# Token stage of a vision tower: three pixel buffers instead of two, and its eight groups written out instead of looped

## The reference

```python
x = img.reshape(B, C, h, P, w, P)                       # 64 images, 14 x 14 patches of 16 x 16 x 3
x = jnp.transpose(x, (0, 2, 4, 3, 5, 1)).reshape(B, h * w, P * P * C)
x = _layernorm(x, ln1_g, ln1_b)                         # over the 768 values of a patch
x = jnp.einsum('bnp,pd->bnd', x, W_proj) + b_proj       # 768 -> 192
x = _layernorm(x, ln2_g, ln2_b)                         # over 192
x = jnp.concatenate([cls, x], axis=1) + pos_embedding
...
h = h + attention(layernorm(h))    # 12 heads, relative positions, 198 tokens an image
h = h + ffn(layernorm(h))          # shared MLP and two of eight experts
```

## Time and profile before

| | |
|---|---|
| median of 3 runs | 5148.42 us (5146.3 to 5152.68) |
| the profiled execution: its time, its span | 5149.14 us, 5147.4 us |
| busy over the span | PE 4691.5 us (91%), DVE 3364.0 (65%), ACT 2283.2 (44%), POOL 562.3 (11%) |
| mean granted clock of TensorE | 0.954 of full speed |
| token stage | from the start to 496 us, where the first instructions of the attention stage stand |
| pixels read | 24 transfers of 1568 KB |

### The profile page before, as it was taken

The page is one execution under the profiler, slowest core; times in us unless marked ns, Lnnn a source line. Parts: engine busy times, 40 slices in busy tenths (PEclk is TensorE's granted clock), DMA queues, the critical chain, the costliest instruction groups (busy, mean ns, idle before and its releaser), DMA issues. The chain is left out here.

```text
span 5147.4 us, 91556 instructions
## 1 busy us (share of the span) xinstructions
PE 4691.5 (91%) x30810; PEld 4419.7 (86%) x30810; DVE 3364.0 (65%) x9549; ACT 2283.2 (44%) x6372; POOL 562.3 (11%) x530
## 2 busy tenths in 40 slices
PE   4775799899899989989989998998999699999999
PEld 4775599899889889989988998998999599999999
DVE  4555566666666766666666666676667477777776
ACT  2443555455555545545555555554554122222222
POOL 1122100000000000000000000000000133333333
PEclk8887799999999999999999999999999799999999
DMA  6452000000000000000000000000000100000000
GB/s 140 97 124 61 13 1 1 1 20 1 1 20 1 1 2 20 1 1 20 1 1 16 6 1 1 20 1 1 11 1 1 38 19 18 18 18 18 18 18 18
DMA packets 65157, 99.50 MB, mean 19 GB/s; under 512 B 3763, under 2 KB 60674, under 8 KB 61120
## 3 DMA queue, kind: packets, MB, share of 16 engines
q1 hardware_dynamic: 61312, 90.31, 7.0%
q0 software_dynamic: 944, 2.42, 0.3%
q10 hardware_dynamic: 2560, 2.36, 0.2%
HBM read 65.88 MB, written 29.20 MB: 18 GB/s over the span
## 5 line engine op out<-in xcount | busy, mean ns | idle before, releaser
L643 ACT ACTIVATE att_prob<-att_s,att_npeak 99x198 f32<-99x198 f32 x1536 | 640.1, 422 | 1221.4 <-DVE att_npeak L816 1175.5
L816 DVE TENSOR_REDUCE att_npeak<-att_s 99x2 f32<-99x396 f32 x768 | 436.0, 568 | 892.3 <-PE att_s L988 890.2
L971 PE MATMUL att_o<-att_probT,att_vx 99*96 99x198 f32 (+1 forms) x3072 | 683.2, 345 | 1.3 <-ACT att_probT L633 1.3
L988 PE MATMUL att_s<-att_kx,att_qx 96*99 96x198 f32 (+1 forms) x3072 | 657.4, 336 | 3.3 <-DVE att_xres L782 2.5
L1356 PE MATMUL ffn_y<-ffn_down,ffn_hidden 128*128 128x192 f32 x3564 | 634.8, 328 | 6.7 <-DVE ffn_acc L1268 4.8
L1356 PEld LDWEIGHTS ffn_y<-ffn_down,ffn_hidden 128*128 128x128 f32 x3564 | 585.6, 190 | 28.4 <-DVE ffn_acc L1268 27.4
L971 PEld LDWEIGHTS att_o<-att_probT,att_vx 99*96 99x96 f32 (+1 forms) x3072 | 509.5, 182 | 42.4 <-issue 32.7
L988 PEld LDWEIGHTS att_s<-att_kx,att_qx 96*99 96x99 f32 (+1 forms) x3072 | 517.1, 168 | 18.4 <-issue 4.4
L806 DVE TENSOR_SCALAR att_prob<-att_prob,att_total 99x198 f32<-99x198 f32 x1536 | 458.9, 342 | 26.9
L1134 POOL TENSOR_TENSOR ffn_hidden<-ffn_relu 128x384 f32<-128x384 f32 x462 | 379.4, 827 | 708.6 <-ACT ffn_relu L1163 400.2
L1163 ACT ACTIVATE ffn_relu<-ffn_h 128x384 f32<-128x384 f32 x231 | 113.3, 490 | 706.2 <-PE ffn_h L1345 705.9
(11 more groups left out here) (201 smaller groups left out, 9368.6 us busy)
## 6 DMA issues: line engine op xcount, KB each, us to landing
tok_pixels<-in_x SPq DMA_DIRECT2D x24, 1568.0 KB
ffn_hid<-hidden SPq DMA_DIRECT2D x34, 288.0 KB, 2.9
att_xres<-hidden SPq DMA_DIRECT2D x8, 1188.0 KB
hidden<-att_xres SPq DMA_DIRECT2D x8, 1188.0 KB
out_hidden<-ffn_acc SPq DMA_DIRECT2D x33, 288.0 KB, 2.3
hidden<-tok_rows SPq DMA_DIRECT2D x8, 1176.0 KB
att_oT<-in_L_attn_qkv_w ACTq DMA_DIRECT2D x1, 1536.0 KB, 11.4
tok_posb<-in_L_tok_pos_embedding POOLq DMA_DIRECT2D x1, 1176.0 KB, 42.6
```

The source lines that it names most:

```text
L643: ins = nc.scalar.activation(prob[:, i % 2, h, :], s_bank[i % 2][0:HALF, h * NTOK:(h + 1) * NTOK], ACT.Exp, bias=npeak[:, i % 2, h:h + 1], ...
L816: nc.vector.tensor_reduce(npeak[:, i % 2, :], s_bank[i % 2][0:HALF, 0:2 * NTOK].rearrange("p (h k) -> p h k", h=2), AX.X, ALU.max, negate= ...
L971: ins = nc.tensor.matmul(o_bank[j % 2][0:M, 0:NTOK], vx[:, p % 2, 2 * b + k, v0:v0 + M], probT[:, j % 2, k * NTOK:(k + 1) * NTOK], start=( ...
L988: ins = nc.tensor.matmul(s_bank[i % 2][0:HALF, h * NTOK:(h + 1) * NTOK], qx[0:K, p % 2, head, q0:q0 + HALF], kx[0:K, p % 2, head, b * NTOK ...
```

## The change

`pixels` gets three buffers and as many semaphores; group g uses buffer g % 3. SP issues three loads at the start and then, after the pixels of group g have been read, the load of g+3. The programs of SP, ACT and DVE in this stage are written out for eight groups instead of looped over pairs. In the last group DVE leaves out the statistics of pixels, their aggregation, scale and shift, and ACT the square root that belongs to them; the pretended arrival goes. PE and POOL keep their loops, and the other stages are as they were.

```diff
+    SLOTS = 3
-        pixels = m.sb("pixels", [P, 2, CH, XROW])
+        pixels = m.sb("pixels", [P, SLOTS, CH, XROW])
...
-                load(0, 0)
-                load(1, 1)
-                with sp.Fori(0, (GROUPS - 2) // 2) as pair:
-                    gg = pair * 2
-                    for s in range(2):
-                        sp.wait_ge(normed_made, (gg + s + 1) * SIDE)
-                        load(gg + s + 2, s)
-                        store(gg + s, s)
-                sp.sem_inc(pixels_in[0], 16 * CH)
-                for s in range(2):
-                    store(GROUPS - 2 + s, s)
+                for g in range(SLOTS):
+                    load(g)
+                for g in range(GROUPS):
+                    if g + SLOTS < GROUPS:
+                        sp.wait_ge(normed_made, (g + 1) * SIDE)
+                        load(g + SLOTS)
+                    store(g, g % 2)
...
-                with act.Fori(0, GROUPS // 2) as pair:
+                for g in range(GROUPS):
+                    s = g % SLOTS
...
+                    if g + 1 < GROUPS:
                         deviation1(g + 2)
-                        act.wait_ge(mv2_made, g + 1)
+                    act.wait_ge(mv2_made, g + 1)
...
-                with dve.Fori(0, GROUPS // 2) as pair:
-                        dve.wait_ge(pixels_in[1 - s], gg * (8 * CH) + 16 * CH * (s + 1))
-                            if wv < SIDE:
-                                ins = statistics1(1 - s, wv)
+                for g in range(GROUPS):
+                    s, more = g % 2, g + 1 < GROUPS
+                    if more:
+                        dve.wait_ge(pixels_in[(g + 1) % SLOTS], 16 * CH * ((g + 1) // SLOTS + 1))
+                        if wv < SIDE and more:
+                            ins = statistics1((g + 1) % SLOTS, wv)
...
+                    if more:
                         dve.wait_ge(normed_made, (g + 1) * SIDE)
                         aggregate(st, mv1, stat1, mv1_made)
-                        aggregate(st, mv2, stat2, mv2_made)
+                    aggregate(st, mv2, stat2, mv2_made)
+                    if more:
                         scale_shift1(st, g + 2)
...
-                        dve.wait_ge(rows_out[s], gg * 8 + PRIMED)
+                    if g >= 2:
+                        dve.wait_ge(rows_out[s], 16 * (g // 2) + PRIMED)
```

More of the change, by code:

```diff
@@ L110, in tokens_stage @@
         y_bank = [m.bank(f"y{v}") for v in range(2)]
-        pixels_in = [m.sem(f"pixels_in{s}") for s in range(2)]
+        pixels_in = [m.sem(f"pixels_in{s}") for s in range(SLOTS)]
         consts_in, weights_in, ident_made = m.sem("consts_in"), m.sem("weights_in"), m.sem("ident_made")
@@ L132, in _, with load @@
                     sp.sem_inc(s, PRIMED)
-                def load(g, s):
+                def load(g):
                     for c in range(CH):
-                        sp.dma_start(pixels[:, s, c, :], x_rows[c, :, bass.ds(g * GB, GB), :]).then_inc(pixels_in[s], 16)
+                        sp.dma_start(pixels[:, g % SLOTS, c, :], x_rows[c, :, g * GB:(g + 1) * GB, :]
+                                     ).then_inc(pixels_in[g % SLOTS], 16)
                 def store(g, s):
                     sp.wait_ge(rows_made, g + 1)
-                    sp.dma_start(hid_rows[:, bass.ds(g * GB, GB), :], rows[:, s, :, :]).then_inc(rows_out[s], 16)
-                load(0, 0)
-                load(1, 1)
-                with sp.Fori(0, (GROUPS - 2) // 2) as pair:
-                    gg = pair * 2
-                    for s in range(2):
-                        sp.wait_ge(normed_made, (gg + s + 1) * SIDE)
-                        load(gg + s + 2, s)
-                        store(gg + s, s)
-                sp.sem_inc(pixels_in[0], 16 * CH)
-                for s in range(2):
-                    store(GROUPS - 2 + s, s)
+                    sp.dma_start(hid_rows[:, g * GB:(g + 1) * GB, :], rows[:, s, :, :]).then_inc(rows_out[s], 16)
+                for g in range(SLOTS):
[5 more added lines that the diff above has]
+                    store(g, g % 2)
                 for s in range(2):
@@ L172, in _ @@
                 deviation1(1)
-                with act.Fori(0, GROUPS // 2) as pair:
[L174 to L188, removed]
+                for g in range(GROUPS):
+                    s = g % SLOTS
+                    act.wait_ge(shift1_made, g + 1)
+                    normalise(s, 0, g * SIDE)
+                    for wv in range(SIDE):
+                        v, t = wv % 2, g * SIDE + wv
+                        if wv + 1 < SIDE:
+                            normalise(s, wv + 1, t + 1)
+                        act.wait_ge(turned, t + 1 + PRIMED)
+                        for i in range(2):
+                            ins = nc.scalar.activation(patchT[:, v, 3 * i:3 * i + 3, :],
+                                                       t_bank[v][i][:, 0:3 * P].rearrange("p (k n) -> p k n", k=3),
+                                                       ACT.Copy)
+                        ins.then_inc(patchT_made, 1)
+                    if g + 1 < GROUPS:
                         deviation1(g + 2)
-                        act.wait_ge(mv2_made, g + 1)
-                        nc.scalar.activation(rstd2[:, :, :], mv2[:, :, 1:2], ACT.Sqrt, bias=eps[0:P, :]).then_inc(sd2_made, 1)
+                    act.wait_ge(mv2_made, g + 1)
+                    nc.scalar.activation(rstd2[:, :, :], mv2[:, :, 1:2], ACT.Sqrt, bias=eps[0:P, :]).then_inc(sd2_made, 1)
             @block.gpsimd
@@ new lines, in _ @@
+                for g in range(GROUPS):
+                    s, more = g % 2, g + 1 < GROUPS
+                    st = Steps(dve, dve_step, 2 + g * PER_GROUP)
+                    if more:
+                        dve.wait_ge(pixels_in[(g + 1) % SLOTS], 16 * CH * ((g + 1) // SLOTS + 1))
+                    dve.wait_ge(rows_normed, g + PRIMED)
+                    for wv in range(SIDE + 1):
+                        t = g * SIDE + wv - 1
+                        if wv:
+                            dve.wait_ge(projected, t + 1)
+                            nc.vector.tensor_tensor(y[:, wv - 1, :], y_bank[(wv - 1) % 2][0:P, 0:DIM], bias[:, :], ALU.add
+                                                    ).then_inc(y_made, 1)
+                        if wv < SIDE and more:
+                            ins = statistics1((g + 1) % SLOTS, wv)
+                            if wv == SIDE - 1:
+                                st.did(ins)
+                        if wv:
+                            dve.wait_ge(y_made, t + 1 + PRIMED)
+                            st.did(nc.vector.bn_stats(stat2[:, wv - 1, :], y[:, wv - 1, :]))
+                    if more:
@@ L288, in _ @@
                         dve.wait_ge(normed_made, (g + 1) * SIDE)
                         aggregate(st, mv1, stat1, mv1_made)
-                        aggregate(st, mv2, stat2, mv2_made)
+                    aggregate(st, mv2, stat2, mv2_made)
+                    if more:
                         scale_shift1(st, g + 2)
-                        dve.wait_ge(sd2_made, g + 1)
-                        st.did(nc.vector.reciprocal(rstd2[:, :, :], rstd2[:, :, :]))
-                        st.settle()
@@ L295, in _ @@
-                        dve.wait_ge(rows_out[s], gg * 8 + PRIMED)
[L296 to L301, removed]
+                    dve.wait_ge(sd2_made, g + 1)
@@ new lines, in _ @@
+                    st.did(nc.vector.reciprocal(rstd2[:, :, :], rstd2[:, :, :]))
+                    st.settle()
+                    if g >= 2:
+                        dve.wait_ge(rows_out[s], 16 * (g // 2) + PRIMED)
+                    for wv in range(SIDE):
+                        ins = nc.vector.tensor_scalar(rows[:, s, wv, :], y[:, wv, :], mv2[:, wv, 0:1], rstd2[:, wv, :],
+                                                      ALU.subtract, ALU.mult)
+                        if wv == SIDE - 1:
+                            ins.then_inc(rows_normed, 1)
@@ L303, in _ @@
+                    assert st.n == (PER_GROUP if more else PER_GROUP - 2), st.n
             @block.tensor
```

## The result

The changed kernel took 5157.42 us (median of 20 runs, 5153.79 to 5161.05), the kernel before 5146.55; the ratio is 1.002, with a 95% interval of 1.0014 to 1.0027. The profiled execution has a span of 5159.1 us. One of the 20 runs of the kernel before took 10713 us, which a median hardly feels. Forecast were 5075 us and a gain of 74. The measurement shows a loss of 11.

What follows compares the result with a forecast made beforehand. PE was taken as the bound, plus 9.10 us a group waiting on late pixels. Savings of 65.5 + 1.5 + 7 = 74.0 us from 5149.14 gave 5075.1, stated as 5075 us, range 5064 to 5092.

Steps and rivals of the forecast that it cites:

- Third buffer: Token stage: loads issued a group earlier remove six of DVE's pixel waits, 77.1 us together; 65.5 us saved.
- the first rival: Start of token stage: three loads share instead of queue, load 1 comes 28.5 us later, total 5103.6 us; 7%.
- Last group: End of token stage: 14 aggregations of unneeded pixel statistics leave the path to the row instructions; 1.5 us saved.
- the template: Old token stage's seventh group window, whose pixel wait was already satisfied: 43.45 us, taken as the model for groups after.
- The granted clock: Group boundaries of the token stage: PE's fall to half clock may cost less; 0 to 14 us gained, 7 taken.
- POOL beside DVE, and both beside the loads: Token stage: POOL's row instructions, DVE's statistics and pixel traffic now coincide without stretching; cost 0.
- The contention rival: Token stage: pixel traffic, POOL and DVE together stretch DVE or transfers, part of the wait returns; 5092 to 5138 us; 8%.
- the lock of the Trainium skill: Port pair shared by DVE and GpSimd, held exclusively: POOL's 11.8 us a group would fall on DVE, 5153 us; 1%.
- Code fetch within the token stage: Written-out DVE and ACT programs need 14 or 15 instruction packets; 0 to 10 us lost, 0 taken.
- The rival of fetches behind pixel packets: Token stage: DVE's and ACT's straight-line code packets queue behind loads, 108 us on the path, 5183 us; 3%.
- Attention and experts must not change by more than some us: Sign to look for in the later stages: their times stay as before within some us.

Runs made afterwards that it cites:

- 8: Changed kernel with 8 small memsets added at the head of DVE's program: 5075.1 us, ratio 0.9868 to the kernel before.
- 64: Changed kernel with 64 small memsets added at the head of DVE's program: 5073.99 us, ratio 0.9858 to the kernel before.
- 100: Changed kernel with 100 small memsets added at the head of DVE's program: 5075.24 us, ratio 0.9868 to the kernel before.
- 112: Changed kernel with 112 small memsets added at the head of DVE's program: 5123.43 us, ratio 0.9961 to the kernel before.
- 128: Changed kernel with 128 small memsets added at the head of DVE's program: 5161.05 us, ratio 1.0032 to the kernel before.
- the loop of 268: Changed kernel with 116 memsets, DVE's experts loop cut from 284 to 268 instructions by leaving out the gates' norming: 5062.91 us, ratio 0.9833.

## Why the prediction was wrong, point by point

- **Third buffer, 65.5 us**: right. All six waits went and the first stayed, at 15.09 us. Load 1 was no later (DVE went on at 65.96 instead of 65.91), so the loads do not share; the first rival falls.
- **Last group, 1.5 us**: right. The last window is 1.51 us shorter than the template (41.94 against 43.45). From the end of the last column's statistics to the group's first row instruction it is 1.85 us, where the kernel before has 3.16. The 14 aggregations left take 1.03 us, and DVE then waits 0.37 for ACT's square root.
- **The granted clock, 7 us**: right in kind, too large. Seven windows take 297.8 us; the template's 43.45 seven times is 304.2. The 6.3 us between them hold the last group's saving too, as the last window ends at its first L295. The six windows before it take 255.9 us against 260.7: the clock gave 4.8, within the bounds of 0 to 14; that it would be half of them was a guess. The windows are not alike, as forecast, but alternate: 43.2 at a mean clock of 0.92, 42.1 at 0.96, as the fall lasts 6.8 us at one boundary and 3.4 at the next. At no boundary did it fail to come, as I had thought possible for some. Windows at the first boundary, at the second, and behind it:

```profile
102.80:109.40 6.60, 5.57 (x22) 5.34 (x23) 5.42 (x18) 5.19 (x8) 2.14 (x1) 0.50 0.88 190
...
147.20:150.40 3.20, 3.20 (x16) 3.06 (x16) 3.16 (x11) 2.68 (x6) 0.00 (x0) 0.50 0.92 202
150.60:155.00 4.40, 4.40 (x34) 4.36 (x34) 2.94 (x10) 2.81 (x5) 4.40 (x1) 1.00 0.86 186
```

  The prediction misread one row. It has the fall at the last boundary of before 0.2 us after PE started again. But a grant of 0.91 over the 3.5 us up to 429.40 means 0.6 us of half clock in them, so the fall came at 428.8, 0.4 us before PE started at 429.18. A fall behind PE's start is seen only after the change, at the second boundary, where it was the short one. There PE started at 147.02, the fall came at 147.1, and the first project took 2.77 us where the template has 4.14:

```profile
147.02 2.47 PE L318 MATMUL tok_t<-tok_ident,tok_normed 112*128 112x112 f32 x12 [4.73 <-ACT tok_normed L166]
149.28 2.77 PE L330 MATMUL tok_y<-tok_w,tok_patchT 128*112 128x192 f32 x12
```

- **The three together**: 65.5, 4.8 and 1.5 us, less 0.7 by which the first window begins later (103.03 instead of 102.33), are the 71.1 us by which the token stage is shorter. 74 were forecast.
- **POOL beside DVE, and both beside the loads, 0**: right. In the group from 231 to 273 us, which has all three at once, L232 takes 412 ns and L215 5906, against 412 and 5897. The contention rival falls, and the lock of the Trainium skill (SBUF — State Buffer, section "SBUF: two separate sides") is again not seen for these instructions. The prediction says that the trace does not agree with the page; that is too strong, as L232 reads one tile and so need not meet the page's condition.
- **Code fetch within the token stage, 0 of 0 to 10 us**: right. 14 or 15 packets were forecast, 11 came up to 425 us (13 by 490), and neither DVE nor ACT has an issue wait there. The forecast divided by 88 working instructions a packet. In this stage the two programs have 965 and 355 instructions of all kinds, and 1320 over 128 is 10.3. The rival of fetches behind pixel packets falls too: the kernel did become slower and by fetches of code, but in the experts stage, which moves no pixels.
- **"Attention and experts must not change by more than some us"**: the step that failed. It stood among the signs to look for, and the sum has it as a zero for which no row is given. I priced the fetching of the code that is written out and not what its length does to the code behind it. In its place the runs show 82 to 85 us: 5.65 us in 15 turns of a loop whose 284 instructions had moved by 95 places of 128. With that undone, the forecast of 5075 stands against 5073.99, 5075.1 and 5075.24. That it is met to 1 us is in part luck: the gain against the kernel before of the same round is 73.1, 70.4 and 70.3 us, where 74 were forecast.

The rule that I cited bears on just this. The Trainium skill, Runtime: NRT & Kernel Launch, section "Instruction fetch mechanics", says that a taken branch whose target is not among the pages held forces a fetch before execution goes on. By that rule every loop that the change does not touch had to be asked whether it still is held; I used it only for the loops that the change removes. The trace agrees with the rule in kind: stalls at the branch's target, 3.0 and 1.7 us. It differs in the unit, which the section gives as 16 KiB blocks for each engine: the packets of q14 are 8192 bytes, and 128 instructions are one turn of the pattern.

What stays open: that three packets are kept and four are not is read from the packet counts and from the places tried (8, 64, 100, 112, 128 and the loop of 268); how the buffer replaces its contents was not tried. In a bad place five packets come per turn, one more than the loop covers; I take the fifth for the one behind the loop, which is argued only. It fits their times: three come at the head, one 30 us later, and one 7 us before the next head. And 3.4 us that the changed kernel lost late in the attention stage are not explained; 2.5 of them had come back at the start of the experts stage, so the loss of 84 us is not touched.

## What to carry to other kernels

A change that alters the number of instructions in one stage moves every later loop of that engine against the ends of the fetched packets; where a loop is about as long as what the engine keeps (here 284 instructions of DVE, by the count kept from 101 places of 128), it can lose a few us in every turn far from the diff. When a gain vanishes in code that was not touched, compare the instruction packets of the two profiles and the "issue" waits at loop heads, and move the code by a few instructions in a stretch where the engine waits anyway: 8 were enough here, 82 us for nothing. And take a verdict on a change only after that, since the same edit is 73 us faster or 11 us slower by its place alone.

## What was not expected of the hardware

A loop of 284 DVE instructions is fetched once, or with five packets of 8192 bytes in every turn, by its place alone: 152 packets in the whole kernel or 226. In the changed kernel the stall is not one but two, 3.0 us at the head and 1.7 us one instruction later, as the packets come 2.4 us apart; with the loop's head 11 or 16 instructions farther from the packet's end only the first is left. In the token stage, straight-line code among pixel traffic at 140 GB/s has no such stall at all. The clock, too, was more regular than thought: with a beat of 42.55 us the half clock lasted 6.8 and 3.4 us in turn, where with 54.4 it lasted 6.8 us at every boundary, and another 10.2 us behind each wait for pixels.
